# Lambda carried by the copies of v, Newton's first value and the places of tokens moved from VectorE to GpSimd

## The reference, cut to what matters

```python
attn1 = causal_attn(q1, k1, vcat, scale)          # vcat: 8 columns per key/value head
attn2 = causal_attn(q2, k2, vcat, scale)
lambda_full = exp(sum(lambda_q1 * lambda_k1)) - exp(sum(lambda_q2 * lambda_k2)) + LAMBDA_INIT
attn = attn1 - lambda_full * attn2
rms = sqrt(mean(attn * attn, axis=-1, keepdims=True) + EPS)
attn = attn / rms * rms_w * (1.0 - LAMBDA_INIT)
x = layernorm(x + attn.reshape(B, T, -1) @ Wo)
logits = x @ router_w + router_b                  # max_prob, max_ind = max, argmax of softmax
out = (silu(a) * g @ w2[e])[max_ind == e] * max_prob    # a, g = halves of x @ w1[e]
x = layernorm(x + out)
```

## Time and profile before

| what | before |
|---|---|
| median of three runs | 677.2 us (674.37 to 679.77) |
| the profiled execution: its time, its span | 680.83 us, 679.0 us |
| busy: TensorE, VectorE, ScalarE, GpSimd | 602.4, 517.0, 426.6, 312.3 us |
| chain that ended last, by engine | PE 60%, DVE 25%, issue 7%, others 2% or less |
| granted TensorE clock, mean over the span | 0.908 |

### The profile page before, as it was taken

The page is one execution under the profiler, slowest core; times in us unless marked ns, Lnnn a source line. Parts: engine busy times, 40 slices in busy tenths (PEclk is TensorE's granted clock), DMA queues, the critical chain, the costliest instruction groups (busy, mean ns, idle before and its releaser), DMA issues.

```text
span 679.0 us, 29739 instructions
## 1 busy us (share of the span) xinstructions
PE 602.4 (89%) x12409; PEld 333.0 (49%) x12409; DVE 517.0 (76%) x1285; ACT 426.6 (63%) x896; POOL 312.3 (46%) x509
## 2 busy tenths in 40 slices
PE   3299999999988998999899999989999898699982
PEld 1145344444533543444344444434444488599972
DVE  2277799998996997799698879967964488756662
ACT  1103688888976886787688778766876435234441
POOL 3222033462865366375535646520534205636674
PEclk9655699999998999899999999986987699899997
DMA  3513313313411331242124114210106443535580
GB/s 122 167 44 100 89 32 90 103 32 79 111 47 43 78 110 37 57 111 75 45 77 109 33 49 111 71 39 25 35 8 218 141 157 126 197 128 192 191 263 21
DMA packets 44486, 63.86 MB, mean 94 GB/s; under 512 B 13440, under 2 KB 35584, under 8 KB 44080
## 3 DMA queue, kind: packets, MB, share of 16 engines
q1 hardware_dynamic: 38816, 54.38, 27.5%
q0 software_dynamic: 2272, 4.69, 1.9%
q10 hardware_dynamic: 3264, 2.89, 1.4%
HBM read 43.88 MB, written 21.65 MB: 97 GB/s over the span
## 4 chain that ended last, share of the span: by engine, by line
PE 60%; DVE 25%; issue 7%; DMA 2%; ACT 2%; POOL 2%; SPq 0%; ACTq 0%; POOLq 0%; DVEq 0%
PE bank L712 16%; DVE mr L1327 15%; PE bank L646 9%; PE bank L628 9%; PE bank L838 7%; PE bank L851 3%; PE bank L720 3%; PE bank L749 3%; PE bank L665 2%; PE bank L723 2%; PE bank L759 1%; DVE rl L1313 1%; DMA rope<-in_c_rope 1%; PE bank L730 1%; PE bank L753 1%
## 5 line engine op out<-in xcount | busy, mean ns | idle before, releaser
L1327 DVE TENSOR_REDUCE mr<-bank 128x8 f32<-128x512 f32 x576 | 369.4, 682 | 75.0 <-PE bank L646 57.6
L909 ACT ACTIVATE work<-bank 128x512 f32<-128x512 f32 x576 | 314.9, 600 | 98.7 <-PE bank L665 79.6
L712 PE MATMUL bank<-work,v_aug 128*32 128x512 f32 (+7 forms) x2048 | 187.1, 443 | 1.6 <-issue 1.6
L646 PE MATMUL bank<-kd,qd 24*64 24x192 bf16 (+7 forms) x2048 | 179.1, 303 | 5.2 <-issue 5.2
L628 PEld LDWEIGHTS bank<-bits 32*64 32x64 bf16 x4608 | 80.5, 107 | 193.5 <-DVE mr L1327 134.2
L665 PE MATMUL bank<-qd,kd 27*64 27x512 bf16 (+7 forms) x2048 | 170.8, 297 | 1.9 <-issue 1.9
L628 PE MATMUL bank<-bits 32*64 32x64 bf16 (+2 forms) x4608 | 137.1, 216 | 30.6 <-DVE mr L1327 14.2
L1086 POOL CAST msplit<-mt 128x32 bf16<-128x32 f32 x32 | 6.8, 211 | 166.5 <-DVE mt L1337 166.4
L838 PE MATMUL bank<-xr,wbuf 128*128 128x256 f32 (+1 forms) x368 | 76.7, 364 | 5.0 <-DVE xr L1582 4.4
L712 PEld LDWEIGHTS bank<-work,v_aug 128*32 128x32 f32 x2048 | 47.7, 112 | 56.5 <-issue 28.4
L646 PEld LDWEIGHTS bank<-kd,qd 24*64 24x64 bf16 x2048 | 70.6, 114 | 9.4 <-issue 9.4
(11 more groups left out here) (182 smaller groups left out, 628.0 us busy)
## 6 DMA issues: line engine op xcount, KB each, us to landing
wbuf<-in_w SPq DMA_DIRECT2D x23, 768.0 KB
qk_parts<-parts SPq DMA_DIRECT2D x90, 128.0 KB, 2.7
kd<-qk_parts SPq DMA_DIRECT2D x64, 96.0 KB
qd<-qk_parts SPq DMA_DIRECT2D x64, 96.0 KB
x_sorted<-in_c_pad SPq DMA_DIRECT2D x9, 390.0 KB, 4.3
xr<-x_sorted SPq DMA_DIRECT2D x16, 130.0 KB
xt_s<-in_xT SPq DMA_DIRECT2D x8, 256.0 KB, 3.9
xn<-in_x SPq DMA_DIRECT2D x7, 256.0 KB
```

Source lines behind the costliest of these rows:

```text
L646: m = pe.matmul(bk[L * c:L * c + L, cols], qd[lo:lo + KROWS, s % 2, second, c, L * n:L * n + L], kd[lo:lo + KROWS, s % 2, second, c, 0:key ...
L712: m = pe.matmul(pv_b[32 * t:32 * t + 32, L * kb:T], v_aug[:, vb, kv + v, kb, :], cols, start=kb == 0, stop=True, skip_group_check=True)
L909: nc.scalar.activation(prob[:, pos, r, :], st_b[no % ST_RING][:, :], ACT.Exp, scale=HD ** -0.5).then_inc(s_sfree, 1)
L1327: V.tensor_reduce(mr[:, s % 2, u % 2, i, i:i + NB], nat_b[no % NAT_RING][:, :].rearrange("p (n t) -> p n t", t=L), AX.X, ALU.max)\
```

## The change

Three things are changed.

1. -lambda is no longer applied to the reciprocals of the second softmax. The copies of v for partitions 64 to 127 (j = 1) are scaled by `lam_n`, which is read as a per-partition value, for batches 1 to 7. For batch 0 the copies are made before lambda is known, so one ScalarE instruction scales them in place when it is; TensorE's first product waits for it.
2. `first_guess` is cut to the sum of squares on VectorE. The rest is two instructions, `nv = (ss + eps) * -0.5`, and the bits of Newton's first value as `bits(nv) * -0.5 + GUESS`; they stand on GpSimd ahead of `inverse_root`, for batch 7 on VectorE in `last_rms`.
3. The places of batches 0 to 6 are worked out on GpSimd just ahead of their scatters, with three additions of halves in place of the reduction. `group` stays in VectorE's queue at the step where it was. Batch 7's places stay on VectorE.

```diff
-NEWTON = 15
+NEWTON = 14
+GUESS = float(0x5F3759DF - 0x00400000 - 0x40000000)
-JOBS = {"weigh": (6, 10, 3), "guess": (7, 4, 5), "stats": (9, 17, 6), "choose": (11, 9, 8), "chance": (12, 0, 2),
-        "place": (12, 8, 3)}
+JOBS = {"weigh": (6, 10, 2), "guess": (7, 4, 1), "stats": (9, 17, 6), "choose": (11, 9, 8), "chance": (12, 0, 2),
+        "place": (12, 10, 1)}
...
+                    if s == 0:
+                        pe.wait_ge(s_vaug, 5)
...
+                        if bn and j:
+                            nc.scalar.activation(dst, of, ACT.Copy, scale=lam_n[L:P, 0:1]).then_inc(done, 1)
+                        else:
+                            nc.scalar.activation(dst, of, ACT.Copy).then_inc(done, 1)
...
+            act.wait_ge(s_lam, 3)
+            act.wait_ge(s_vaug, 4)
+            second = v_aug[L:P, 0, :, :, VW:VW + 2 * HD].rearrange("p k n v -> p (k n) v")
+            nc.scalar.activation(second, second, ACT.Copy, scale=lam_n[L:P, 0:1]).then_inc(s_vaug, 1)
...
             def inverse_root(b):
 
                 n = NEWTON * b
+                wait(pool, s_ss, b + 1)
+                nc.gpsimd.tensor_scalar(nv[:, :], ss[:, :], 2 * HD * RMS_EPS, -0.5, ALU.add, ALU.mult).then_inc(s_newton, 1)
+                wait(pool, s_newton, n + 1)
+                nc.gpsimd.tensor_scalar(rinv[:, :].bitcast(I32), nv[:, :].bitcast(I32), -0.5, GUESS, ALU.mult, ALU.add)\
+                    .then_inc(s_newton, 1)
...
+            def places(b):
+
+                wait(pool, s_rt, RT_STEPS * b + 10)
+                emptied(pool, "rank", b)
+                nc.gpsimd.tensor_tensor(place_f[:, :, :], coded[:, :, :], chosen[:, b % 2, :, :], ALU.mult)\
+                    .then_inc(s_rt, 1)
+                pool.wait_ge(s_rt, RT_STEPS * b + 11)
+                nc.gpsimd.tensor_tensor(place4[:, :, :], place_f[:, :, 0:4], place_f[:, :, 4:8], ALU.add)\
+                    .then_inc(s_place, 1)
+                pool.wait_ge(s_place, 2 * b + 1)
+                nc.gpsimd.tensor_tensor(place2[:, :, :], place4[:, :, 0:2], place4[:, :, 2:4], ALU.add)\
+                    .then_inc(s_place, 1)
+                pool.wait_ge(s_place, 2 * b + 2)
+                nc.gpsimd.tensor_tensor(pos_f[:, :], place2[:, :, 0], place2[:, :, 1], ALU.add).then_inc(s_rt, 1)
+                pool.wait_ge(s_rt, RT_STEPS * b + 12)
+                nc.gpsimd.tensor_copy(pos_u[:, NI * b:NI * b + NI], pos_f[:, :]).then_inc(s_pos, 1)
...
                     if b is not None:
+                        places(b)
                         sort(b)
...
-            def first_guess(b, k):
-
-                n = NEWTON * b
-                if k == 0:
-                    wait(dve, s_post, 4 * b + 3)
-                    wait(dve, s_newton, n)
-                    V.tensor_reduce(ss[:, :], sq[:, :, :], AX.X, ALU.add).then_inc(s_ss, 1)
-                elif k == 1:
-                    wait(dve, s_ss, 2 * b + 1)
-                    V.tensor_scalar(ss[:, :], ss[:, :], 2 * HD * RMS_EPS, None, ALU.add).then_inc(s_ss, 1)
...
+            def square_sums(b):
+
+                wait(dve, s_post, 4 * b + 3)
+                wait(dve, s_newton, NEWTON * b)
+                V.tensor_reduce(ss[:, :], sq[:, :, :], AX.X, ALU.add).then_inc(s_ss, 1)
...
-                else:
-                    wait(dve, s_rl, 3 * b + 2)
-                    second = rl[:, :].rearrange("p (n j) -> p n j", j=2)[:, :, 1]
-                    V.tensor_scalar(second, second, lam_n[:, 0:1], None, ALU.mult).then_inc(s_rl, 1)
...
             def place_of(b, k):
 
+                if b < B - 1:
+                    if b in GROUP_BATCH:
+                        group(GROUP_BATCH.index(b))
+                    return
```

More of the change, by code:

```diff
@@ L273, in build @@
         ss = sb("ss", [P, NI * KVH * 2])
-        nint = sb("nint", [P, NI * KVH * 2], I32)
         nv = sb("nv", [P, NI * KVH * 2])
@@ L296, in build @@
         place_f = sb("place_f", BT)
+        place4 = sb("place4", [P, NI, NX // 2])
+        place2 = sb("place2", [P, NI, NX // 4])
         rmax = sb("rmax", [P, NI])
@@ L413, in build @@
         s_total = sem("s_total")
+        s_place = sem("s_place")
         s_pos = sem("s_pos")
@@ L915, in take_v @@
                     for h in range(2):
[L916 to L919, removed]
+                        dst = v_aug[L * j:L * j + L, bn % 2, :, h:NB:2, VW * j:VW * j + 2 * HD]
+                        of = src[L * h:L * h + L, 0:NI * L].rearrange("p (i k v) -> p k i v", k=KVH, v=2 * HD)
+                        if bn and j:
+                            nc.scalar.activation(dst, of, ACT.Copy, scale=lam_n[L:P, 0:1]).then_inc(done, 1)
+                        else:
+                            nc.scalar.activation(dst, of, ACT.Copy).then_inc(done, 1)
             def take(name, n):
@@ L1097, in over_total @@
             def over_total(b):
-                wait(pool, s_rl, 3 * b + 3)
+                wait(pool, s_rl, 2 * b + 2)
                 wait(pool, s_post, 4 * b)
@@ L1118, in inverse_root @@
                 n = NEWTON * b
+                wait(pool, s_ss, b + 1)
[3 more added lines that the diff above has]
+                    .then_inc(s_newton, 1)
                 for k in range(3):
-                    m = n + 3 + 4 * k
+                    m = n + 2 + 4 * k
                     wait(pool, s_newton, m)
@@ L1321, in row_max @@
+            def weigh(b, k):
+                emptied(dve, "turn_ot", SUPER * b + SUPER - 1)
+                i = slice(NI // 2 * k, NI // 2 * k + NI // 2)
+                V.reciprocal(rl[:, 2 * NH // 2 * k:2 * NH // 2 * (k + 1)],
+                             on_s[:, i, :, :, :].rearrange("p i k r (j v) -> p (i k r j) v", v=VW)[:, :, 2 * HD])\
+                    .then_inc(s_rl, 1)
             def row_max(s, u):
@@ L1417, in place_of @@
                     V.tensor_copy(pos_u[:, NI * b:NI * b + NI], pos_f[:, :]).then_inc(s_pos, 1)
-                    if b in GROUP_BATCH[:2]:
-                        group(GROUP_BATCH.index(b))
             def job(name, b, k):
@@ L1424, in job @@
                 elif name == "guess":
-                    first_guess(b, k)
+                    square_sums(b)
                 elif name == "stats":
@@ L1539, in last_difference @@
             def last_difference():
-                wait(dve, s_rl, 3 * B)
+                wait(dve, s_rl, 2 * B)
                 wait(dve, s_post, 4 * b7)
@@ L1551, in last_rms @@
             def last_rms():
+                n = NEWTON * b7
+                wait(dve, s_ss, B)
+                V.tensor_scalar(nv[:, :], ss[:, :], 2 * HD * RMS_EPS, -0.5, ALU.add, ALU.mult).then_inc(s_newton, 1)
+                wait(dve, s_newton, n + 1)
+                V.tensor_scalar(rinv[:, :].bitcast(I32), nv[:, :].bitcast(I32), -0.5, GUESS, ALU.mult, ALU.add)\
+                    .then_inc(s_newton, 1)
                 for k in range(3):
-                    m = NEWTON * b7 + 3 + 3 * k
+                    m = NEWTON * b7 + 2 + 3 * k
                     wait(dve, s_newton, m)
@@ L1561, in last_rms @@
                         .then_inc(s_newton, 1)
-                wait(dve, s_newton, NEWTON * b7 + 12)
+                wait(dve, s_newton, NEWTON * b7 + 11)
                 emptied(dve, "turn_attn", b7 - 1)
@@ L1627, in _ @@
             gate(1)
-            for k in range(JOBS["guess"][2]):
-                first_guess(b7, k)
+            square_sums(b7)
             last_rms()
@@ L1647, in _ @@
             take("rank", b7)
-            for k in range(JOBS["place"][2]):
+            for k in range(3):
                 place_of(b7, k)
```

16 lines of the change are left out of this document (removed).

## The result

| | before | after |
|---|---|---|
| median, 14 runs each on one chip | 677.6 us (668.9 to 685.7) | 685.7 us (679.6 to 695.6) |
| ratio, 95% interval | | 1.0129 (1.008 to 1.0178) |
| profiled execution: time, span, clock | 680.8, 679.0, 0.908 | 686.0, 684.2, 0.906 |
| busy DVE, ACT, POOL | 517.0, 426.6, 312.3 | 513.2, 430.2, 322.0 |

Ratios leave out each kernel's runs that lie over 1.5% above its fastest; medians, means and mean clocks are over all runs. The forecast was 676.9 us and no change. VectorE lost 3.8 us of work, as meant, and its share of the chain that ended last went from 25% to 23%, but the kernel got slower.

A forecast was written before the change was run, and what follows sets the result against it. The chain was taken as mostly TensorE with a quarter of VectorE, TensorE's low clock a second cost. VectorE's steps -1.6 and scaled copies +1.3 gave -0.3 us on 677.2: 676.9 us, range 670.1 to 682.0.

The forecast's parts named there:

- The step that failed: Places on GpSimd: scatters start 0.1 to 0.8 us earlier, batch 4's about 3; nothing gained or lost.
- Rival C: Clock's low stretches move, either sign: 1.3 us a short one, 4.2 a long one; 681.1 or 670.1; chance 0.16.
- Part 1's copies: Scaled copies of v on ScalarE, batches 2 to 7: 0.107 us more for each of twelve, 1.3 us lost.
- VectorE's steps: Third weigh and four guess steps go: batch 0 0.56 us, batches 1 to 6 0.5, tail 0.56; 1.6 gained.
- The tail's guess: Batch 7's guess on VectorE: four steps in 0.79 us become two of about 0.25 each, 0.29 us gained.
- Newton on GpSimd: Two new instructions at most 0.4 to 0.8 us each, covered; GpSimd's wait before Newton 2 to 3 us shorter.
- ScalarE's scaling of batch 0's copies: Some 0.7 us plus a wait for lambda, about 1 us together; cost nothing, 1 us if cover were gone.
- Rival B: Scaled copies cost more than VectorE gives, from 0.13 us each; at the upper bound 678.2 us; chance 0.16.
- A: Rival: VectorE's time comes off in full, batches 0 to 6 and tail; -3.2 us, 674.0; chance 0.13.
- The chance of 0.13 for over 1% faster: Whole kernel below 670.4 us, needing VectorE's time off in full together with a gain from fewer low clock stretches.
- The range: Whole kernel's time, 670.1 to 682 us: fewer low clock stretches below, one long one more and 0.9 us above.

The follow-up runs named there:

- e13: Part 3 alone on the kernel before, in a starving session: ratio 1.0226, median 688.1 against 675.8 us.
- e14: Parts 1 and 2 without part 3, against the kernel before, in a starving session: ratio 1.0015, median 675.6 against 675.8 us.
- e11: The kernel before with VectorE's place steps two steps earlier, against the kernel before, in a starving session: ratio 1.0150, median 688.2 against 678.6 us.
- e16: The changed kernel with scatters of batches 0 to 4 held until VectorE's step 11, against the kernel before: ratio 1.0064, median 681.2 against 674.8 us.
- e15: The whole change against the kernel before, in a starving session: ratio 1.0189, median 687.0 against 675.8 us.
- e2: Parts 1 and 2 without part 3, against the kernel before, in a free session (no starving): ratio 1.0082, median 651.2 against 648.9 us.
- e17: The kernel before with part 2 and the sum of squares in two halves, against the kernel before: ratio 0.9911, median 668.8 against 674.8 us.
- e10: The kernel before with the sum of squares in two halves, against the kernel before: ratio 1.0027, median 677.4 against 678.6 us.
- e1: Part 3 alone on the kernel before, in a free session (no starving): ratio 1.0010, median 647.9 against 648.9 us.

## Why the prediction was wrong, point by point

- **The step that failed** is in part 3: "The change moves this stretch and does not shorten it: nothing gained or lost". The stretch moved by 0.54 us, inside my 0.1 to 0.8 (for batch 4 by 2.6), and three phases got 1.1 to 1.7 us longer. The term put at nothing was thus the whole loss. I had the starving and the low clock in hand as rows, and I did not join them: where the clock falls depends on when TensorE starves. Part 3 has all of the loss in starving sessions (1.0226 in e13 against 1.0015 in e14). That an earlier start can bring such a loss is shown (e11: 1.4 us earlier, places left on VectorE, 1.5%). Beside it, the traces show a deeper starving with the places on GpSimd, 3.1 and not 4.0 us of TensorE's work in a scatter; its cause, and its share of the loss, stay open.
- **Rival C** named the mechanism with the wrong lean. Its price of 1.3 us for a short low stretch stood up (5.6 against 4.3 us in e11). The 4.2 us for a long one did not: it set the 18.7 us phase behind batch 4's against 14.5 us, but that phase has fewer matmuls (389 against 421) and takes 12.9 us at full clock (e16), so the stretch cost 5.8. I gave the rival mostly to the faster side, "since less starving is more likely than more". In the event the mean clock fell, from 0.915 to 0.897 (e15). "Against it: the scatters, the longest such, stay" was the fault: they do not stay, they move.
- **Part 1's copies**: 107 ns was forecast for each scaled copy; it is 499 against 382 ns long, and costs the chain 0.09 us more for each of twelve copies in six pairs, 1.1 us: right. The Trainium skill, page "ScalarE: Activation LUTs", section "What ACT_TABLE_LOAD costs", puts a pointer operand at some 93 ns; the trace agrees on the chain, with 0.09 us.
- **VectorE's steps**: batches 1 to 3 gained nothing where 0.12 us each was forecast (14.4 us phases as before at full clock; the idle wait before the row maxima grew from 0.42 to 0.73 us). Batch 0's guess gave 0.3 us (12.7 to 12.4) and not 0.4, and the third weigh step 0.05 and not 0.16. The tail's guess was right at 0.33 for 0.29. For parts 1 and 2 the sum is near nothing, as forecast: 1.0015 in e14, and 651.0 against 651.2 us at a clock of 0.92 in e2.
- **Newton on GpSimd**: the waits fell from 36.5 to 11.7 us, 3.5 us a batch where 2 to 3 were forecast; its two new instructions take 0.24 us each, below my 0.4 to 0.8.
- **ScalarE's scaling of batch 0's copies** takes 0.79 us behind a wait of 0.28, about 1 us as forecast, and no cost of it shows: the phase without jobs takes 12.5 us against 12.4, and e14, which has it too, is level with before.
- **Rival B** (copies at 0.13 us or more each) did not occur, nor did A (phases shorter along with VectorE's work). The chance of 0.13 for over 1% faster was too high even by my own rows: it asked for A together with C's gain, and A alone had 0.13.
- **The range** (670.1 to 682.0) left out the measured 685.7, since it allowed for one long low stretch more, 4.2 us. A mean clock lower by 0.018 costs some 7 us at 4 us for each 0.01.

## What to carry to other kernels

When a kernel's clock is not full, a change has to be priced twice: once at full clock, and once by what it does to the stretches in which TensorE starves, because 0.01 of mean clock went with 4 us here. Taking work off an engine is not worth anything by itself; ask what starts earlier by it, and on what that start falls. Here part 2 and one 0.68 us reduction cut in two halves three steps apart gained 0.9% (e17), where all three edits together lost 1.3%. The halves without part 2 gained nothing that could be measured (e10), since they moved other work into the way.

## What the runs showed of the hardware that I had not expected

- While GpSimd issues four indirect DMAs of 128 rows (4.9 us), TensorE and ScalarE are starved in some sessions (54 matmuls, 3.06 us busy in e13) and not in others (136 matmuls, 4.90 us busy in e1), with the same program and on the same chip. The kernel before takes 28 us less in the second kind (649 and 677 us), of which five scatter phases at 4.0 us make 20. What distinguishes the sessions isn't known.
- A VectorE instruction with two inputs in SBUF (128 x 32) that fell among GpSimd's rotations took 1.31 us (e10) or 0.55 us (e11) and not 0.18, and ended within 0.05 us of the end of a rotation.
- The two instructions of the first guess on integers and floats (64 columns) take GpSimd 0.24 us each, less than a float addition of 64 columns (0.38).
- The lead of a scatter (from its row numbers to its start) is 0.82 us behind GpSimd's own `pos_u` and about 0.83 behind VectorE's, but 0.18 us behind its last input where its row numbers had long been there.
